# The histogram's one-hots of a chunk from one comparison instead of 14, in a graph network layer on one core

## The reference

```python
edge_input = concat([x[src], x[dst], edge_attr])         # 50000 x 272
m   = silu(silu(edge_input @ eW1 + eb1) @ eW2 + eb2)     # 50000 x 128
agg = segment_sum(m, src, 50000)                         # add each edge's row to its source node
upd = silu(concat([x, agg]) @ nW1 + nb1) @ nW2 + nb2
out = layernorm(x + (x + upd))
```

## Time and profile before

| | |
|---|---|
| median of 3 runs | 1612.81 us (1610.55 to 1620.77) |
| profiled execution, first to last instruction | 1611.9 us (the only time given for it) |
| TensorE busy | 1213.7 us, 75% |
| VectorE busy | 780.3 us, 48% |
| ScalarE busy | 458.8 us, 28% |
| GpSimd busy | 1023.1 us, 63% |
| DMA | 352.97 MB, mean 219 GB/s; the fill's queue 68.32 MB with the output |
| mean granted TensorE clock | 0.930 |

### The profile page before, as it was taken

The page is one execution under the profiler, slowest core; times in us unless marked ns, Lnnn a source line. Parts: engine busy times, 40 slices in busy tenths (PEclk is TensorE's granted clock), DMA queues, the critical chain, the costliest instruction groups (busy, mean ns, idle before and its releaser), DMA issues.

```text
span 1611.9 us, 24482 instructions
## 1 busy us (share of the span) xinstructions
PE 1213.7 (75%) x6825; PEld 873.1 (54%) x6825; DVE 780.3 (48%) x3182; ACT 458.8 (28%) x846; POOL 1023.1 (63%) x1267
## 2 busy tenths in 40 slices
PE   1224487778788787888878887877877869999995
PEld 1224255545455454555555544544545559888884
DVE  7448434433443434434344333333333439888885
ACT  0000111122222222222222221211222227777775
POOL 7471745555556565555555665666666548998996
PEclk9999888999999999999988997998999979999998
DMA  9991443456666566565555655654655349999994
GB/s 379 413 413 40 134 151 119 135 159 191 186 186 198 176 189 190 178 191 182 182 183 178 181 177 155 183 179 142 195 168 166 90 138 399 411 413 412 411 406 180
DMA packets 175501, 352.97 MB, mean 219 GB/s; under 512 B 30350, under 2 KB 81855, under 8 KB 175364
## 3 DMA queue, kind: packets, MB, share of 16 engines
q1 hardware_dynamic: 128740, 230.97, 43.4%
q10 hardware_dynamic: 21600, 68.32, 10.6%
q0 software_dynamic: 25024, 52.10, 10.2%
HBM read 235.21 MB, written 116.06 MB: 218 GB/s over the span
## 4 chain that ended last, share of the span: by engine, by line
PE 41%; another core or an unknown queue 19%; issue 15%; DVE 7%; POOL 6%; ACTq 6%; DMA 3%; ACT 1%; POOLq 0%; SPq 0%; DVEq 0%
PE psum L658 11%; ACTq L763 6%; PE psum L702 5%; PE psum L681 4%; PE psum L732 4%; PE psum L704 4%; PE psum L689 3%; DMA ring<-table 3%; PE psum L700 3%; PE psum L714 3%; PE psum L646 3%; POOL windows L613 2%; PE psum L747 2%; DVE same L993 2%
## 5 line engine op out<-in xcount | busy, mean ns | idle before, releaser
L539 POOL DMA_INDIRECT table<-qs,pos x391 | 387.8, 992 | 361.6 <-DVE qs L1021 262.5
L496 POOL DMA_INDIRECT ring<-x_d,idx_src x391 | 380.5, 973 | 169.9 <-issue 117.8
L658 PE MATMUL psum<-work,windows 128*128 128x128 f32 x1568 | 241.6, 319 | 173.3 <-issue 164.7
L658 PEld LDWEIGHTS psum<-work,windows 128*128 128x128 f32 x1568 | 228.6, 229 | 244.3 <-issue 244.3
L977 DVE COPY work<-psum 128x512 f32<-128x512 f32 x98 | 67.8, 691 | 471.4 <-remote 300.1
L732 PE MATMUL psum<-work,ring 128*128 128x80 f32 x1250 | 157.5, 280 | 26.6 <-DVE work L1041 22.4
L732 PEld LDWEIGHTS psum<-work,ring 128*128 128x128 f32 x1250 | 149.6, 196 | 35.4 <-issue 22.7
L1021 DVE COPY qs<-psum 128x512 f32<-128x512 f32 x98 | 67.6, 690 | 188.2 <-remote 174.9
L681 PE MATMUL psum<-xT_in,w_self 128*128 128x320 f32 x314 | 128.7, 495 | 24.4 <-issue 19.6
L784 ACT COPY u_out<-psum 128x320 f32<-128x320 f32 x129 | 54.9, 426 | 290.4 <-remote 242.5
L773 ACT COPY work<-psum 128x512 f32<-128x512 f32 x98 | 57.4, 586 | 277.2 <-PE psum L658 194.3
(11 more groups left out here) (120 smaller groups left out, 1572.0 us busy)
## 6 DMA issues: line engine op xcount, KB each, us to landing
windows<-x_d SPq DMA_DIRECT2D x392, 128.0 KB
ring<-table SPq DMA_DIRECT2D x79, 528.0 KB, 10.6
table<-empty ACTq DMA_DIRECT2D x9, 4224.0 KB
edge_rows<-edges_dram SPq DMA_DIRECT2D x98, 384.0 KB
xT_in<-xT_d SPq DMA_DIRECT2D x78, 320.0 KB
out<-windows ACTq DMA_DIRECT2D x78, 320.0 KB, 6.1
u_dram<-u_out SPq DMA_DIRECT2D x64, 320.0 KB
own_x<-x_d SPq DMA_DIRECT2D x48, 320.0 KB, 8.3
```

Source lines behind the costliest of these rows:

```text
L496: pool.indirect_dma_start(rows, None, x[:, :], bass.IndirectOffsetOnAxis(ap=idx[:, g * TILES + t:g * TILES + t + 1], axis=0)).then_inc(don ...
L539: pool.indirect_dma_start(table[:, :], bass.IndirectOffsetOnAxis(ap=pos[:, g * TILES + t:g * TILES + t + 1], axis=0), q[g % Q][:, t, :], None,
L658: last = nc.tensor.matmul(p_dst[:, t * P:(t + 1) * P], window[g % WINDOWS][:, t, r * D:(r + 1) * D], pick[g % 2][:, r, t * P:(t + 1) * P], ...
```

## The change

The 14 one-hots of a chunk are made by one comparison with two tensor inputs: the constant `chunk_ids` (each of 0 to 124 repeated 14 times) against the chunk's 14 values of `coarse`, repeated 125 times. Within a home the order changes from column-major to id-major: the 14 columns of one id lie side by side, so the weights of one matmul are 125 elements 28 bytes apart. `chunk_ids` comes from an iota on GpSimd, ahead of its gathers; `coarse_h` is `coarse` in 16 bits and takes the place of the conversion of `coarse_ids`. `own_homes` becomes one home, so HOMES is 17, and with it the first pause waits for 11 chunks.

```diff
-            coarse_ids = tmp("coarse_ids", [P, COARSES], F16)
+            chunk_ids = tmp("chunk_ids", [P, COARSES * CHUNK], F16)
+            coarse_h = tmp("coarse_h", [P, COLS], F16)
...
-            own_homes = tmp("own_homes", [P, 2 * CHUNK * COARSES], F16)
+            own_homes = tmp("own_homes", [P, CHUNK * COARSES], F16)
...
-                is_coarse.append(tile[:, k * CHUNK * COARSES:(k + 1) * CHUNK * COARSES].rearrange("p (c f) -> p c f", f=COARSES))
+                is_coarse.append(tile[:, k * CHUNK * COARSES:(k + 1) * CHUNK * COARSES].rearrange("p (f c) -> p f c", c=CHUNK))
...
+            pool.iota(chunk_ids[:], [[1, COARSES], [0, CHUNK]], base=0, channel_multiplier=0,
+                      allow_small_or_imprecise_dtypes=True).then_inc(s_chunk_ids, 1)
...
-                last = nc.tensor.matmul(p_count[c // BANK_COLS][0:COARSES, o:o + FINE], is_coarse[c // CHUNK % HOMES][:, c % CHUNK, :],
+                last = nc.tensor.matmul(p_count[c // BANK_COLS][0:COARSES, o:o + FINE], is_coarse[c // CHUNK % HOMES][:, :, c % CHUNK],
                                         is_fine[:, c, :], start=True, stop=True)
...
-            V.tensor_copy(coarse_ids[:], bucket_i[:]).then_inc(s_plan, 1)
+            V.tensor_copy(coarse_h[:], coarse[:, 0:COLS]).then_inc(s_plan, 1)
             dve.wait_ge(s_plan, 17)
-            for c in range(COLS):
-                if c % CHUNK == 0 and c >= HOMES * CHUNK:
-                    dve.wait_ge(s_count_mm, c // CHUNK - HOMES + 1)
-                last = V.tensor_scalar(is_coarse[c // CHUNK % HOMES][:, c % CHUNK, :], coarse_ids[:], coarse[:, c:c + 1], None,
-                                       ALU.is_equal)
-                if c % CHUNK == CHUNK - 1:
-                    last.then_inc(s_is_coarse, 1)
+            dve.wait_ge(s_chunk_ids, 1)
+            for k in range(COLS // CHUNK):
+                if k >= HOMES:
+                    dve.wait_ge(s_count_mm, k - HOMES + 1)
+                cols = coarse_h[:, k * CHUNK:(k + 1) * CHUNK]
+                V.tensor_tensor(is_coarse[k % HOMES], chunk_ids[:].rearrange("p (f c) -> p f c", c=CHUNK),
+                                cols.unsqueeze(1).to_broadcast([P, COARSES, CHUNK]), ALU.is_equal).then_inc(s_is_coarse, 1)
```

More of the change, by code:

```diff
@@ L166, in gnn_kernel @@
                                (windows[:, :].bitcast(F16), WINDOWS * TILES * 2 * D * 4), (edge_rows, ROWS_IN * 6 * GROUP),
-                               (own_homes, 4 * CHUNK * COARSES)):
+                               (own_homes, 2 * CHUNK * COARSES)):
             for k in range(bytes_in // (2 * CHUNK * COARSES)):
-                is_coarse.append(tile[:, k * CHUNK * COARSES:(k + 1) * CHUNK * COARSES].rearrange("p (c f) -> p c f", f=COARSES))
+                is_coarse.append(tile[:, k * CHUNK * COARSES:(k + 1) * CHUNK * COARSES].rearrange("p (f c) -> p f c", c=CHUNK))
         HOMES = len(is_coarse)
@@ L200, in gnn_kernel @@
             sem(n) for n in ("s_idx_src", "s_idx_dst", "s_src_i", "s_dst_i", "s_weights"))
-        s_slot_i, s_iota, s_consts, s_ident, s_empty, s_fill = (
-            sem(n) for n in ("s_slot_i", "s_iota", "s_consts", "s_ident", "s_empty", "s_fill"))
+        s_slot_i, s_iota, s_chunk_ids, s_consts, s_ident, s_empty, s_fill = (
+            sem(n) for n in ("s_slot_i", "s_iota", "s_chunk_ids", "s_consts", "s_ident", "s_empty", "s_fill"))
         s_plan, s_ids, s_is_fine, s_is_coarse, s_count_mm, s_sums, s_before_tile, s_worst, s_fit_mm, s_fits_i = (
```

## The result

The changed kernel takes 1621.19 us in the median of 20 runs (1613.12 to 1631.29), the kernel before 1615.34 in 20 runs made together with it (1606.52 to 1622.59). The ratio is 1.004, 95% interval 1.0023 to 1.0058: 6 us slower, where 10 us faster was forecast. It is inside the 1%, but clear of noise and on the other side.

What follows compares the result with a forecast made beforehand. The histogram's end was taken to release everything behind it; fed PE at 0.113 us a matmul, less slower gathers and the iota, ends it at 145.3 for 155.6, gaining 10.3 us: 1602 us, range 1591 to 1629.

Steps and rivals of the forecast that it cites:

- I take 0.113: PE in the histogram: strided weight loads cost nothing extra, 0.113 us per matmul; called a choice and the main doubt.
- The upper bound: PE's strided weight load, from DVE's strided read: 0.22 us per load, 0.44 if that read used two ports.
- the 18.7 us of the prediction's rival: Histogram's end: how far it moves later if a matmul takes 0.22 us instead of 0.113.
- thin stretch: Histogram, twice, 40 us each: DVE and PE together get about 104 instructions per 40 us; cause not named.
- The first rival: Matmuls outside thin stretches: strided weights cost, 1621 us at 0.22 us each (chance 0.25), 1672 at 0.44 (0.11).
- The first thin stretch: Histogram, 29.60 to 69.16 us before: expected to last to 75.2 with 46 matmuls, 99 done.
- The iota was put at 1.67 us: GpSimd, ahead of all gathers: one more iota of 1750 elements a partition, 1.67 us.
- A comparison of 1.07 us: DVE in the histogram: one 128x1750 comparison takes 1.07 us if halfwords go twice as fast, else 1.98.
- the 0.44 read from the f32 operations: GpSimd's gathers beside DVE's long comparisons: each 0.44 us slower, ten gathers 4.4 us.
- the final batch behind the last matmul: GpSimd's final 24 gathers wait for the last histogram matmul, so the 10.3 us gain is all on the path.
- the gap from the histogram's end to the first SiLU: From the last histogram matmul to ACT's first SiLU: unchanged at 40.7 us.
- the third rival: Thin stretches: PE doesn't inherit DVE's share, keeps 34 matmuls; 7 us off, 1606; counted within the forecast's 0.49.

Runs made afterwards that it cites:

- e8: Changed kernel with CHUNK = 4 instead of 14, so weights lie 8 bytes apart: 1330.4 us (one run), where the kernel before takes 1326.8.
- e10: e7's kernel again (adjacent weights, one comparison a chunk in pairs), against the kernel before at 1326.75 us: ratio 1.0072.
- e1: Kernel before with one comparison a chunk, column-major, so weights stay adjacent and no iota for the ids: 1581.5 us, ratio 0.9843.
- e12: e1's kernel again, where the kernel before takes 1326.75 us: ratio 1.0125.
- e2: Changed kernel with chunk_ids copied by DVE instead of the iota on GpSimd: 1606.2 us, ratio to the kernel before 1.0017.
- e3: Kernel before with both of GpSimd's pauses taken out: 1620.8 us (one run).
- e5: Kernel before without pauses, with a memset of 640 elements behind each of the first 48 gathers; before takes 1326.8 us: ratio 1.0196.
- e9: e5's kernel again, where the kernel before takes 1326.75 us: ratio 1.0198.
- f3: e5's kernel once more, where the kernel before takes 1325.1 us: 1354.1 us.
- g1: e5's kernel a last time, on the kind of chip where the kernel before takes about 1327 us: ratio 1.0197.
- e7: Kernel before with one column-major comparison a chunk, values stored twice and compared in pairs, weights adjacent; before takes 1326.8 us: ratio 1.0058.

## Why the prediction was wrong

**The step that failed** is "I take 0.113": a matmul with its weights 28 bytes apart takes 0.226 us. The upper bound, from a strided read on another engine, had it at 0.22; I set it aside for the overlap of the loads, and the overlap didn't cover it. e8 shows that it is the distance: at 8 bytes nearly all of the cost is gone. (By the Trainium skill, SBUF — State Buffer, the note on "cachelines", consecutive accesses to the same 16-byte line run at full bandwidth and each new line pays a penalty; 0.118 us at 8 bytes and 0.226 at 28 agree with it, and give the penalty's size for this weight load.)

The step weighs more than the 18.7 us of the prediction's rival. 392 loads at 0.113 us less are 44 us; from 25.0 on, adjacent weights would have ended the histogram near 69 us, ahead of the 80.6 at which the thin stretch began (an estimate; e10, with such loads and comparisons on the second kind, ended at 66.4). But the comparisons would then have ended earlier too, and the gathers been 1.25 us apart sooner, so how much of it would have been gained on the first kind is not shown.

**The first rival** had the right mechanism and nearly the right size, 8 us slower, for 4 us in the histogram's end and 6 in the time. That its 1621 us is the median measured is luck: the base had moved from 1612.8 to 1615.3; its working put 53 matmuls into the 8.65 us up to 29.6, where at 0.22 us each 39 fit, which would make its end some 3 us later; and its path was not this one, since two more steps were off:
- The first thin stretch was taken as a fixture, with its start set by counted instructions. It did not come. With DVE's comparisons holding the gathers to 1.96 us and then 1.57, PE went on at its own pace to 80.6 us. That gave 247 matmuls where the rival's working had about 125 by then, and cancelled much of the stride's cost. e1 has both thin stretches gone from the histogram, one coming behind it, and gains 23 us; its comparisons are hardly cheaper (1.9 us a chunk for 2.3), and e12 shows that the same edit gains nothing where no thin stretch is.
- The iota was put at 1.67 us from one of 1536 elements; it took 4.50 us, and slowed DVE's copies beside it. That is 5.6 us on GpSimd. e2 undoes it: 4 us off the histogram's end.

**What held.** A comparison of 1.07 us, to the digit; that DVE's comparisons slow the gathers, though by 0.71 us each (1.66 + 0.30 us beside them) and not by the 0.44 read from the f32 operations; the final batch behind the last matmul; the gap from the histogram's end to the first SiLU, 40.5 us for 40.7. (The Trainium skill, SBUF — State Buffer, section Who interferes with whom, has DVE's second pair of ports shared with GpSimd under an exclusive lock, and an operation with two SBUF inputs contend with a GpSimd instruction that reads SBUF, as the gather does for its indices; 0.94 us becoming 1.66 beside a two-tensor comparison agrees.) PE did not get DVE's share in the thin stretch, as the third rival said: 25 matmuls in 51.6 us, at one each 2.8 us, with DVE idle. Taking the 104 instructions per 40 us of the earlier trace rows as one supply for both was wrong. That PE made even fewer than its 34 in 40 us fits the rows of before, where it waited for a chunk of one-hots and then ran many at once, which the rival had not seen:

```profile
39.79 1.55 PE L629 MATMUL psum<-is_fine,work 128*125 128x5 f16 x13 [9.03 <-remote]
```

The prediction also gives the DMA's 1.03 for both thin stretches, where the earlier trace rows has 0.86 in the second; no term of the sum uses it.

**Where the expected gain went.** DVE's one-hots did become cheap, 28 us of work for 64. On the first kind the pace went over to PE, whose loads took twice as long, and a thin stretch came back 20 us after DVE had stopped hindering GpSimd. On the second kind GpSimd never waited for the histogram: its issue sets the time from 4 us on, and what the change does to it there is to hinder it.

**Open.** Why the runs on one chip have thin stretches and those on four have not. What it is that takes about 1.4 us for a gather, if the estimate from the tails is right, and holds DVE and PE to one instruction in that time: that it is not the DMA's traffic e3 shows, and no view names it. What the strided loads alone cost in time on the first kind: e8's form, which cures them, ran only on the second. Whether spacing alone cures it with before's comparisons: e5, e9, f3 and g1 never ran on a chip of the first kind, and e1, where only longer comparisons spaced the gathers, is the only case of a histogram freed of it. On the second kind no version beat the kernel before.

## What to carry to other kernels

Measure a strided weight load before building on it: f16 weights 8 bytes apart cost next to nothing here, 28 bytes apart they doubled the time of a short matmul. So write the layout that the weights need and let DVE pay. e7 gets adjacent weights and the fast comparison by storing values in pairs, and was still 0.6% slower than before; beside its comparisons a gather takes 1.67 us for 0.94. Long two-tensor operations on DVE and iotas on GpSimd are not free beside GpSimd's indirect DMAs: count their queue before DVE's busy time. And see a small ratio on more than one chip before believing its mechanism: the same edit is 1.6% faster in e1 and 1.25% slower in e12.

## What the runs showed of the hardware that was not expected

- The same kernel takes 1605 to 1615 us in some groups of runs and 1326 in others, on different chips, with the same DMA load up to 86 us and the clock at 1.00 in the histogram of both (means 0.930 and 0.959). In the first, while GpSimd's gathers come every 1.25 us and 6 to 14 us longer, DVE and PE fall to one instruction per 1.40 us each, a weight load counting as one; in the second they run at full pace beside the same gathers.
- An f16 iota of 128x1750 takes 4.50 us, of 128x500 (e8) 1.16 us, of 1x1536 1.47 us, and DVE's copy of eight elements beside the first took 5.13 us.
- A two-tensor comparison on f16 takes 1.07 us for 1750 elements if all operands have an innermost step of one (pairs included, 1.0 us for 1764 at start-to-start), and about 1.9 us if one repeats a value innermost.
